# Second attention with its scores formed twice, and the last two experts by token halves

## The chip, the core and the metric

The kernel runs on one core of a Trainium2 chip. That core has a matrix engine (TensorE, PE in the rows, with its weight loads as PEld), a vector engine (VectorE, DVE), an activation engine (ScalarE, ACT), a general engine (GpSimd, POOL) and a queue engine for transfers (SyncE, SP). Each runs its own list of instructions in order and waits on semaphores for the others. The metric is the device time of one execution in microseconds; less is better.

## What is computed

Eight sequences of 128 tokens with 128 channels go through four residual layers: a cross attention with 8 heads, a mixture of 8 experts with 2 chosen per token, a second cross attention with 16 heads of 8 channels, and a three-layer network with weights of +1 and -1. The part that the change is about, from the reference:

```python
def _L1_xattn_ref(x, context, Wq, bq, Wk, bk, Wv, bv, Wo, bo):
    N_HEADS = 16; D_EMBED = 128; D_HEAD = 8
    q = split_heads(x @ Wq + bq)
    k = split_heads(context @ Wk + bk)
    v = split_heads(context @ Wv + bv)
    scores = jnp.einsum('bhqd,bhkd->bhqk', q, k) / np.sqrt(D_HEAD)
    attn = jax.nn.softmax(scores, axis=-1)
    out = jnp.einsum('bhqk,bhkd->bhqd', attn, v)
    return out.transpose(0, 2, 1, 3).reshape(B, S, D_EMBED) @ Wo + bo
x = x + _L0_ffn_ref(_layernorm(x), ...)      # 8 experts, hidden size 256
x = x + _L1_xattn_ref(_layernorm(x), ctx_768, ...)
x = x + _L1_ffn_ref(_layernorm(x), ...)
```

## The kernel before

The program is written by hand, engine by engine: each block lists its engine's instructions in their order, and semaphores join them. Nothing is scheduled by a tool. "Batch" is one sequence of 128 tokens; a "token half" is four batches.

The experts are worked through as 16 pieces q = 0 to 15, expert q // 2 and token half q % 2. TensorE forms the hidden values (`b_hidden`, 12 products of 512 columns), ScalarE applies the SiLU (L895), VectorE multiplies by the gate (`b_gate`, L1212), TensorE goes back to 128 channels (`b_down`, L616), and VectorE adds the result, weighted for each token, to `x_sb` (`b_add`, L1219). In between TensorE forms the keys of the second attention (`k1_keys`), which end in `k_st`: of its 128 rows each head owns 8, each value split into parts (32 rows for a head, so 4 heads in a group `g`, and 4 groups). After the last piece VectorE normalises the four batches of the first half (`ln_root`, `ln_scale`, L1071), TensorE turns them, and `c_queries` forms the queries of four groups for 512 tokens, which ScalarE and VectorE put into `q_all` (`c_query_signed` L936, `c_query_stack` L1302).

The second attention has 32 units, one for each batch and group of four heads. GpSimd spreads the keys of a batch into a block-diagonal form, `k_bd` (`stage_k`, L388), so that one product over all 128 rows gives the scores of four heads (`c_scores`, L693, one of 512 columns). VectorE takes the maximum over the keys (L1311) and subtracts it (L1315), ScalarE takes the exponential (L945), TensorE turns the four 128x128 tiles (`c_turn`, L700), ScalarE copies them out (L950), and TensorE multiplies by the values (`c_values`, L716). The column of ones in `v_a` gives the sum of the exponentials. After four units comes a tail: copy (L955), turn back (L724), division (L1322, L1324), turn (L728), copy (L958), output product (L731), residual and statistics (L1329, L1024). The loop `c_step` works on two batches at a time.

The last network needs a normalised first token half, which GpSimd makes beside the last units (`ln_root` and `ln_scale` on GpSimd, L301 to L316), then `d_unit` (L757) with its evacuations on ScalarE (L981, L987) and VectorE (L1366, L1375). TensorE also has filler products (`keep_clock`, L431: 128x128 products of `ones`), which compute nothing.

## Time and profile before

| | us |
|---|---|
| runs shown, median | 261.87 |
| lowest and highest of the 3 | 260.78 and 262.34 |
| profiled execution, its own time | 261.25 |
| profiled execution, span of the core | 259.5 |

The profile is one execution. Its span is 1.75 us shorter than the time of that same execution; the rest lies around it. TensorE is busy for 92% of the span, VectorE for 73%, ScalarE for 57%, GpSimd for 35%. In the chain of work that ended last, TensorE has 49%, VectorE 27% and ScalarE 8%. By stage, the first attention lies at about 18 to 72 us, the experts at 72 to 157, the second attention at 157 to 232, and the last network reaches to the end. The ends of matrix products are modelled in such a profile, so TensorE looks busy where it may only be draining: starts are safer to read than ends.

### The profile page before, as it was taken

The page shows a single profiled execution, that of the slowest core. Times are in us where ns is not written, and L with a number is a line of the kernel's source. Part 1 is how long each engine was busy: PE and PEld are TensorE (multiplying, and loading weights), DVE is VectorE, ACT ScalarE, POOL GpSimd, SP SyncE. Part 2 cuts the span into 40 slices and gives each one's busy share as a digit, 9 for nine tenths or more (in the row PEclk, how much of TensorE's full clock was granted, in tenths as well). Part 3 has the DMA queues.
Part 4 walks back from the last instruction along what each step waited for, and adds up shares of the span by engine and source line. Part 5 has one row for each costly group of instructions (what it writes and reads, how often), then busy time and mean ns, then how long its engine had stood idle before and what let it go on. Part 6 is the DMA issues. An engine that isn't in the chain of part 4 may idle for free.

```text
span 259.5 us, 5047 instructions
## 1 busy us (share of the span) xinstructions
PE 237.5 (92%) x1726; PEld 185.0 (71%) x1726; DVE 190.7 (73%) x472; ACT 146.8 (57%) x346; POOL 90.4 (35%) x108
## 2 busy tenths in 40 slices
PE   8979798897989999999999999788999998798994
PEld 7346678787967889889889997555655554466782
DVE  0799977776579855655665689977999999568862
ACT  2643968879655432232232144776777777656841
POOL 3352594040402032131269503643655525230200
PEclk9999999999999999999999999999999999999998
DMA  7940010000000012012010000000000000000002
GB/s 200 211 121 4 0 42 3 0 3 0 3 0 3 28 35 61 19 42 61 15 46 23 0 0 1 3 1 3 0 0 3 0 3 0 4 0 0 0 3 81
DMA packets 11243, 6.59 MB, mean 25 GB/s; under 512 B 2772, under 2 KB 10904, under 8 KB 11224
## 3 DMA queue, kind: packets, MB, share of 16 engines
q1 hardware_dynamic: 11224, 6.33, 9.0%
q8 instruction: 12, 0.20, 0.3%
q14 instruction: 7, 0.06, 0.1%
HBM read 5.81 MB, written 0.52 MB: 24 GB/s over the span
## 4 chain that ended last, share of the span: by engine, by line
PE 49%; DVE 27%; issue 8%; ACT 8%; DMA 2%; POOL 2%; DVEq 1%; SPq 0%; ACTq 0%
PE ps L616 10%; PE ps L435 8%; PE ps L437 7%; PE ps L436 7%; PE ps L757 7%; DVE negmax L1311 6%; ACT probs L846 3%; PE ps L526 3%; PE ps L506 3%; DVE xn L1071 2%; DMA x_sb<-in_x 2%; DVE probs L1315 2%; DVE h_c L1302 2%; ACT part L936 1%; DVE stats L1024 1%
## 5 line engine op out<-in xcount | busy, mean ns | idle before, releaser
L895 ACT ACTIVATE kT<-ps 128x512 f32<-128x512 f32 x32 | 19.1, 598 | 43.7 <-PE ps L437 43.6
L388 POOL TENSOR_TENSOR k_bd<-k_st,block_of 128x2048 fp32r<-128x2048 f32 x8 | 28.8, 3602 | 20.1 <-PE ps L693 20.1
L616 PE MATMUL ps<-w,kT 128*128 128x128 f32 x256 | 31.1, 275 | 0.0
L616 PEld LDWEIGHTS ps<-w,kT 128*128 128x128 f32 x256 | 30.4, 192 | 0.7
L1212 DVE TENSOR_TENSOR kT<-ps,kT 128x512 f32<-128x512 f32 x32 | 21.8, 689 | 11.1 <-PE ps L437 8.8
L435 PE MATMUL ps<-xT_hi,w_hi 128*128 128x512 f32 x64 | 26.6, 416 | 0.7 <-issue 0.6
L364 POOL TENSOR_TENSOR w_hi<-w_raw,zero 128x512 fp32r<-128x512 f32 x8 | 8.3, 1040 | 51.6 <-DMA w_raw<-in_L_ffn_W 37.3
L945 ACT ACTIVATE probs<-probs 128x512 f32<-128x512 f32 x32 | 20.0, 629 | 11.0 <-DVE probs L1315 11.0
L437 PE MATMUL ps<-xT_hi,w_lo 128*128 128x512 f32 x64 | 25.2, 393 | 0.0
L436 PE MATMUL ps<-xT_lo,w_hi 128*128 128x512 f32 x64 | 25.0, 390 | 0.0
L1219 DVE SCALAR_TENSOR_TENSOR x_sb<-ps,comb,x_sb 128x128 f32<-128x128 f32 x64 | 18.0, 343 | 9.4 <-PE ps L616 9.4
L1315 DVE TENSOR_TENSOR probs<-ps,negmax 128x512 f32<-128x512 f32 x32 | 22.1, 692 | 3.1
L846 ACT ACTIVATE probs<-ps,negmax 128x128 f32<-128x128 f32 x64 | 22.7, 420 | 1.8 <-DVE negmax L1137 1.8
L700 PE MATMUL ps<-ident,probs 128*128 128x128 f32 x128 | 20.2, 280 | 1.9 <-ACT probs L945 1.6
L1311 DVE TENSOR_REDUCE negmax<-ps 128x4 f32<-128x512 f32 x32 | 21.7, 679 | 0.0
L700 PEld LDWEIGHTS ps<-ident,probs 128*128 128x128 f32 x128 | 14.4, 140 | 7.9 <-ACT probs L945 7.1
L950 ACT ACTIVATE probsT<-ps 128x512 f32<-128x512 f32 x32 | 18.7, 584 | 0.4 <-PE ps L700 0.4
L846 ACT ACTIVATION_READ_ACCUMULATOR probs<-ps,negmax 128x1 f32 x64 | 16.6, 260 | 0.0
L693 PE MATMUL ps<-k_bd,h_c 128*128 128x512 f32 x32 | 15.2, 481 | 0.3 <-DVE h_c L1302 0.3
L435 PEld LDWEIGHTS ps<-xT_hi,w_hi 128*128 128x128 f32 x64 | 12.1, 188 | 3.2 <-issue 0.7
L437 PEld LDWEIGHTS ps<-xT_hi,w_lo 128*128 128x128 f32 x64 | 12.0, 188 | 2.8
L716 PE MATMUL ps<-probsT,qo 128*32 128x128 f32 x256 | 13.6, 285 | 0.4 <-DVE h_c L1302 0.4
(189 smaller groups left out, 533.5 us busy)
## 6 DMA issues: line engine op xcount, KB each, us to landing
w_raw<-in_L_ffn_W SPq DMA_DIRECT2D x16, 128.0 KB, 2.2
w<-in_L_ffn_W SPq DMA_DIRECT2D x8, 128.0 KB, 2.2
x_sb<-in_x SPq DMA_DIRECT2D x1, 512.0 KB, 5.6
out<-qo SPq DMA_DIRECT2D x2, 256.0 KB, 2.3
ctx_sb<-in_ctx SPq DMA_DIRECT2D x1, 384.0 KB, 3.5
w_raw<-in_L_xattn_Wq SPq DMA_DIRECT2D x1, 256.0 KB, 5.8
wo<-in_L_xattn_Wo SPq DMA_DIRECT2D x1, 256.0 KB, 5.6
k_i<-in_L_ffn_k SPq DMA_DIRECT2D x1, 256.0 KB, 3.5
```

The lines of the kernel that those rows point to most:

```text
L388: pool.tensor_tensor(k_bd[:, j, :, :, :], keys, blocks, ALU.mult).then_inc(c_k, 1)
L435: pe.matmul(dst, w_hi, x_hi, start=start, stop=False)
L436: pe.matmul(dst, w_hi, x_lo, start=False, stop=False)
L437: return pe.matmul(dst, w_lo, x_hi, start=False, stop=stop)
L616: ins = pe.matmul(ps[:, 4 + slot, k * C:(k + 1) * C], uT[:, slot, c, k * P:(k + 1) * P], w3[:, buf, c, :], start=(c == 0), stop=(c == NH - 1))
L700: ins = pe.transpose(ps[:, 4 + u % 2, h * P:(h + 1) * P], sh1[:, u % 4, h * P:(h + 1) * P], ident[:, :])
L846: ins = act.activation(probs[:, j, h, :], ps[:, 2 * j + h % 2, (h // 2) * P:(h // 2 + 1) * P], ACT.Exp, bias=negmax[:, j, h:h + 1], scale= ...
L895: act.activation(silu[:, c, :], ps[:, c, :], ACT.Silu).then_inc(b_silu, 1)
L945: act.activation(sh1[:, u % 4, :], sh1[:, u % 4, :], ACT.Exp, scale=D1 ** -0.5).then_inc(c_exp, 1)
L1212: dve.tensor_tensor(uT[:, slot, c, :], ps[:, 2 + c, :], silu[:, c, :], ALU.mult).then_inc(b_u, 1)
L1311: dve.tensor_reduce(negmax1[:, u % 4, :], src, X, ALU.max, negate=True).then_inc(c_max, 1)
L1315: dve.tensor_tensor(sh1[:, u % 4, :].rearrange("p (h k) -> p h k", k=P), src, negmax1[:, u % 4, :].unsqueeze(2).to_broadcast([P, 4, P]), A ...
```

## The change

The second attention forms its scores twice. The first time they have the queries along the partitions; VectorE reduces them only to the maximum. The negated maxima are placed in `top_w` (zero elsewhere), TensorE turns `top_w`, and VectorE adds the result to the queries: the maximum thus stands as one further row of each head, and the keys have 1.0 in that row. The second product has the keys along the partitions, gives the shifted and already turned scores, and ScalarE writes their exponential straight to where the value product reads it. Block-diagonal keys, subtraction, turning and copy of the exponentials are gone. To free the row, the repeated weights of the queries and keys are zero in one of the four parts (`NS - 1`).

Both score products work on 32 rows at a time, so the head's own rows, at `tile_position` (32r, 0); a "half" `a` is two of the four heads of every group, 8 products of 128 columns, in order g, r, so that two row groups take turns and write to different banks.

The loop over the steps `s` is new on all engines. In step `s` TensorE forms the shifted scores of batch `s`, the first scores of batch `s + 2`, turns the maxima of batch `s + 1`, multiplies values of batches `s - 1` and `s`, and does parts of the tails of `s - 1` and `s - 2`. Two banks hold first scores, two hold shifted scores.

The last two experts, 6 and 7, are worked through as: 6 on the first half, 7 on the first half, 6 on the second half, 7 on the second half. The core of the diff:

```diff
-            def stage_k(b, j):
-                keys = f32(k_st[:, :, bass.ds(b * P, P)]).unsqueeze(2).to_broadcast([P, NG, 4, P])
-                blocks = block_of[:, :].unsqueeze(1).unsqueeze(3).to_broadcast([P, NG, 4, P])
-                pool.tensor_tensor(k_bd[:, j, :, :, :], keys, blocks, ALU.mult).then_inc(c_k, 1)
...
+            pool.memset(top_w, 0.0).then_inc(zeros_ok, 1)
...
+                    pe.wait_ge(b_lo, E)
+                    b_hidden(i * 4 + 5, 1, 0)
...
             b_down(q, 0, 0, NP - 1)
-            pe.wait_ge(b_lo, E)
-            b_hidden(q + 2, 1, 0)
-            b_down(q + 1, 1, 0, NP - 1)
-            b_down(q + 2, 0, 1, NP - 1)
+            b_hidden(q + 2, 0, 1)
+            b_down(q + 1, 1, 1, NP - 1)
             b_hidden(q + 3, 1, 1)
-            keep_clock(5, M0 + 1)
+            b_down(q + 2, 0, 0, NP - 1)
             b_down(q + 3, 1, 1, NP - 1)
...
-                pe.matmul(ps[:, g, :], q, k_bd[:, j, g, :, :].rearrange("p h k -> p (h k)"),
-                          start=True, stop=True).then_inc(c_s, 1)
...
+                for g in range(NG):
+                    for r in (2 * a, 2 * a + 1):
+                        rows, bs = slice(32 * r, 32 * r + 32), slice(b * P, (b + 1) * P)
+                        ins = pe.matmul(ps[:, S_BANK + r % 2, g * P:(g + 1) * P], q_all[rows, g, bs], k_st[rows, g, bs],
+                                        start=True, stop=True, tile_position=(32 * r, 0))
...
+            def c_shifted(b, a):
+
+                if a == 0:
+                    pe.wait_ge(c_qa, b + 1)
+                if 2 * b + a > 0:
+                    pe.wait_ge(c_exp, 2 * b + a)
...
+                        ins = pe.matmul(ps[:, E_BANK + r % 2, g * P:(g + 1) * P], k_st[rows, g, b * P:(b + 1) * P],
+                                        q_sh[rows, b % 2, g * P:(g + 1) * P], start=True, stop=True,
+                                        tile_position=(32 * r, 0))
...
+            def c_step(s):
+                if s < NB:
+                    c_shifted(s, 0)
+                if s + 2 < NB:
+                    c_scores(s + 2, 0)
+                if s == 0:
+                    c_queries(NG + 2)
+                if s + 1 < NB:
+                    c_turn_max(s + 1)
+                if s >= 2:
+                    c_tail(s - 2, 1)
+                if 1 <= s <= NB:
+                    c_values(s - 1, 1)
+                if s == NB:
+                    d_unit(0)
+                if s < NB:
+                    c_shifted(s, 1)
+                if s + 2 < NB:
+                    c_scores(s + 2, 1)
+                if s < NB:
+                    c_values(s, 0)
...
+            def c_exp_half(b, a):
+                act.wait_ge(c_st, 2 * b + a + 1)
+                act.activation(p1T[:, a, :, :, :].rearrange("p r g q -> p r (g q)"), ps[:, E_BANK:E_BANK + 2, :], ACT.Exp,
+                               scale=D1 ** -0.5).then_inc(c_exp, 1)
...
                 dve.wait_ge(masks, 8)
+                dve.tensor_scalar(is_lo[:, 1:2], is_lo[:, 1:2], 1.0, None, ALU.is_equal).then_inc(masks, 1)
...
+            def c_top(b, a):
+
+                dve.wait_ge(c_s, 2 * b + a + 1)
+                top = top_w[:, b % 2, :, :].rearrange("p g (r m) -> p r g m", r=4)[:, 2 * a:2 * a + 2, :, 3 * D1]
+                dve.tensor_reduce(top, ps[:, S_BANK:S_BANK + 2, :].rearrange("p r (g k) -> p r g k", g=NG), X, ALU.max,
+                                  negate=True).then_inc(c_max, 1)
+
+            def c_shift(b):
+
+                dve.wait_ge(c_w, b + 1)
+                dve.tensor_tensor(q_sh[:, b % 2, :].rearrange("p (g q) -> p g q", g=NG),
+                                  ps[:, W_BANK, :].rearrange("p (g q) -> p g q", g=NG),
+                                  f32(q_all[:, :, b * P:(b + 1) * P]), ALU.add).then_inc(c_qa, 1)
```

VectorE at the end of the experts, before: L1219 is `b_add` (four for a piece), L1212 `b_gate`, L1024 the statistics, L1071 the normalised tokens.

```order
L1212 TENSOR_TENSOR kT<-ps,kT 128x512 x2
L1219 SCALAR_TENSOR_TENSOR x_sb<-ps,comb,x_sb 128x128 x8
L1024 BN_STATS stats<-x_sb 128x6 x4
L1212 TENSOR_TENSOR kT<-ps,kT 128x512 x2
L1038 BN_AGGR meanvar<-stats 128x2 x4
...
L1071 TENSOR_SCALAR xn<-x_sb,meanvar,rs 128x128 x4
L1219 SCALAR_TENSOR_TENSOR x_sb<-ps,comb,x_sb 128x128 x4
```

The same place now (L1251 is `b_add`, L1244 `b_gate`, L1054 the statistics, L1101 the normalised tokens):

```order
L1244 TENSOR_TENSOR kT<-ps,kT 128x512 x2
L1251 SCALAR_TENSOR_TENSOR x_sb<-ps,comb,x_sb 128x128 x4
L1054 BN_STATS stats<-x_sb 128x6 x4
L1244 TENSOR_TENSOR kT<-ps,kT 128x512 x2
L1068 BN_AGGR meanvar<-stats 128x2 x4
...
L1251 SCALAR_TENSOR_TENSOR x_sb<-ps,comb,x_sb 128x128 x4
L1101 TENSOR_SCALAR xn<-x_sb,meanvar,rs 128x128 x4
L1251 SCALAR_TENSOR_TENSOR x_sb<-ps,comb,x_sb 128x128 x4
```

One addition of a piece has moved from before the statistics to between the root and the normalised tokens.

TensorE in the steady part of the attention, before, one batch: L693 scores, L700 turns of the exponentials, L716 values, L731, L724 and L728 the tails.

```order
L693 MATMUL ps<-k_bd,h_c 128x512
L700 MATMUL ps<-ident,probs 128x128 x4
L716 MATMUL ps<-probsT,qo 32x128 x4
L731 MATMUL ps<-wo,o1T 128x128
L693 MATMUL ps<-k_bd,h_c 128x512
...
L724 MATMUL ps<-ident,ov 128x128 x4
```

The same place now, one step: L701 shifted scores, L688 first scores, L714 turns of the maxima, L729 values, L746, L742 and L754 the tails.

```order
L701 MATMUL ps<-h_a,k_st 128x128 x8
L688 MATMUL ps<-k_st,h_c 128x128 x8
L714 MATMUL ps<-ident,probs 128x128 x4
L746 MATMUL ps<-ident,o 128x128
L729 MATMUL ps<-probsT,qo 32x128 x8
L701 MATMUL ps<-h_a,k_st 128x128 x8
L688 MATMUL ps<-k_st,h_c 128x128 x8
L729 MATMUL ps<-probsT,qo 32x128 x8
L742 MATMUL ps<-ident,ov 128x128 x4
L754 MATMUL ps<-wo,o1T 128x128
```

Of a batch's 4 score products, 16 turns of exponentials and 16 value products, 32 score products of 32 rows, 4 turns of maxima and 16 value products remain. Each fence above counts instructions as written; a full-precision product of 128 columns shows as two in the rows.

VectorE in the same step now: L1342 the maxima of a half, L1348 the shift, L1356 and L1360 the division, L1366 the residual.

```order
L1342 TENSOR_REDUCE probs<-ps 128x2x4
L1348 TENSOR_TENSOR h_a<-ps,h_c 128x512
L1342 TENSOR_REDUCE probs<-ps 128x2x4
L1356 RECIPROCAL rsum<-ps 128x16
L1360 TENSOR_TENSOR o<-ps,rsum 128x4x4x8
L1366 TENSOR_TENSOR x_sb<-ps,x_sb 128x128
L1054 BN_STATS stats<-x_sb 128x6
```

Before, the same stretch held four pairs of maximum and subtraction:

```order
L1311 TENSOR_REDUCE negmax<-ps 128x4
L1315 TENSOR_TENSOR probs<-ps,negmax 128x512
...
L1322 RECIPROCAL rsum<-ps 128x16
L1324 TENSOR_TENSOR o<-ps,rsum 128x128
...
L1329 TENSOR_TENSOR x_sb<-ps,x_sb 128x128
```

## Rows read from the trace of the kernel before

**Rows 1.** The page: span and busy time of each engine

```profile
span 259.5 us, 5047 instructions
...
PE 237.5 (92%) x1726; PEld 185.0 (71%) x1726; DVE 190.7 (73%) x472; ACT 146.8 (57%) x346; POOL 90.4 (35%) x108
```

**Rows 2.** Two stages: length, busy us of PE, PEld, DVE, ACT, POOL, clock

```profile
163.00:183.00 20.00, 16.89 (x130) 11.26 (x129) 16.40 (x27) 14.26 (x27) 9.90 (x13) 1.00 0.00 1
183.00:215.00 32.00, 30.29 (x292) 18.12 (x290) 29.28 (x60) 24.39 (x48) 14.67 (x5) 1.00 0.00 1
```

**Rows 3.** Chain that ended last: start us, duration us, what

```profile
198.03 0.29 DVE x_sb L1329
...
204.72 0.29 DVE x_sb L1329
```

**Rows 4.** Groups by line: count | busy us, mean ns | idle before

```profile
L388 POOL TENSOR_TENSOR k_bd<-k_st,block_of 128x2048 fp32r<-128x2048 f32 x8 | 28.8, 3602 | 20.1 <-PE ps L693 20.1
...
L1315 DVE TENSOR_TENSOR probs<-ps,negmax 128x512 f32<-128x512 f32 x32 | 22.1, 692 | 3.1
...
L1311 DVE TENSOR_REDUCE negmax<-ps 128x4 f32<-128x512 f32 x32 | 21.7, 679 | 0.0
...
L945 ACT ACTIVATE probs<-probs 128x512 f32<-128x512 f32 x32 | 20.0, 629 | 11.0 <-DVE probs L1315 11.0
...
L950 ACT ACTIVATE probsT<-ps 128x512 f32<-128x512 f32 x32 | 18.7, 584 | 0.4 <-PE ps L700 0.4
...
L1137 DVE TENSOR_REDUCE negmax<-ps 128x8 f32<-128x1024 f32 x8 | 9.8, 1223 | 4.7 <-PE ps L494 4.6
...
L981 ACT ACTIVATE k_bd<-ps,scale 128x512 fp32r<-128x512 f32 x8 | 5.4, 692 | 4.3 <-PE ps L757 4.3
```

**Rows 5.** TensorE in order of time: start us, duration us, instruction

```profile
202.16 0.48 PE L693 MATMUL ps<-k_bd,h_c 128*128 128x512 f32 x1
202.48 0.60 PE L700 MATMUL ps<-ident,probs 128*128 128x128 f32 x4
203.01 0.43 PE L716 MATMUL ps<-probsT,qo 128*32 128x128 f32 x8
203.36 0.49 PE L731 MATMUL ps<-wo,o1T 128*128 128x128 f32 x2
```

**Rows 6.** TensorE in order of time, first attention

```profile
47.31 1.16 PE L494 MATMUL ps<-kT,qo 64*128 64x128 f32 x16
48.40 0.33 PE L517 MATMUL ps<-probsT,v 128*64 128x128 f32 x2
```

**Rows 7.** All engines in order of time, first queries

```profile
163.88 1.90 PE L431 MATMUL ps<-ones 128*128 128x128 f32 x16
...
164.74 0.74 DVE L1302 SCALAR_TENSOR_TENSOR h_c<-ps,is_lo,part 128x512 fp32r<-128x512 f32 x1
```

**Rows 8.** Order of time, end of the experts

```profile
145.98 3.74 PE L616 MATMUL ps<-w,kT 128*128 128x128 f32 x32
...
152.59 0.69 DVE L1212 TENSOR_TENSOR kT<-ps,kT 128x512 f32<-128x512 f32 x1 [0.21 <-PE ps L437]
...
155.59 1.41 DVE L1071 TENSOR_SCALAR xn<-x_sb,meanvar,rs 128x128 f32<-128x128 f32 x4
...
156.92 1.11 DVE L1219 SCALAR_TENSOR_TENSOR x_sb<-ps,comb,x_sb 128x128 f32<-128x128 f32 x4
```

**Rows 9.** Order of time, end of the attention

```profile
215.64 0.17 DVE L1047 TENSOR_SCALAR rs<-nt 128x4 int32<-128x4 int32 x1
...
218.80 3.15 POOL L316 TENSOR_SCALAR xn<-x_sb,meanvar,rs 128x128 f32<-128x128 f32 x4
...
231.96 0.29 DVE L1024 BATCH_NORM_STATS2 stats<-x_sb 128x6 f32<-128x128 f32 x1
...
233.01 0.69 DVE L1375 TENSOR_TENSOR k_bd<-kT,k_bd 128x512 fp32r<-128x512 f32 x1
```

**Rows 10.** Order of time, the masks before the experts

```profile
79.40 0.17 DVE L1120 TENSOR_SCALAR sign<-is_lo 128x3 f32<-128x3 f32 x1
```

More of the change, by code:

```diff
@@ L199, in program @@
         stored = sem("stored")
-        const_ok, split_w0, split_w1, masks = (sem(n) for n in (
-            "const_ok", "split_w0", "split_w1", "masks"))
+        const_ok, zeros_ok, split_w0, split_w1, masks = (sem(n) for n in (
+            "const_ok", "zeros_ok", "split_w0", "split_w1", "masks"))
         pool_step = sem("pool_step")
@@ L636, in _, with b_pair @@
             b_hidden(1, 0, 1, (1,))
-            with pe.Fori(0, NP - 1) as i:
+            def b_pair(i, last):
                 b_down(i * 4, 0, 0, i)
@@ new lines, in c_turn_max, with c_values @@
+            def c_turn_max(b):
+                pe.wait_ge(c_max, 2 * b + 2)
+                if b >= 1:
+                    pe.wait_ge(c_qa, b)
+                if b >= 4:
+                    pe.wait_ge(c_x, b - 3)
+                for g in range(NG):
+                    ins = pe.transpose(ps[:, W_BANK, g * P:(g + 1) * P], top_w[:, b % 2, g, :], ident[:, :])
+                ins.then_inc(c_w, 1)
+            def c_values(b, a):
+                pe.wait_ge(c_exp, 2 * b + a + 1)
+                if a == 0:
@@ L780, in _ @@
-            pe.wait_ge(masks, 12)
+            def c_step(s):
[19 more added lines that the diff above has]
+                    c_values(s, 0)
+                if s == 0:
+                    c_queries(NG + 3)
+                if 1 <= s <= NB:
+                    c_tail(s - 1, 0)
+                if s == NB - 1:
+                    ln_transposes(3, 0)
+                if s >= NB:
+                    d_unit(2 * (s - NB) + 1)
+                if s >= 2:
+                    c_tail(s - 2, 2)
+                if s == NB:
+                    d_unit(2)
@@ L911, in _ @@
             b_silu_step(1)
-            act.wait_ge(masks, 9)
+            act.wait_ge(masks, 10)
             k1_signed(0, 0)
@@ L935, in c_query_signed @@
                     act.wait_ge(k1_st, NK1 - 1 + n)
-                act.activation(part[:, n % 2, :], ps[:, n if n < NG else M0 + 1, :], ACT.Copy,
+                act.activation(part[:, n % 2, :], ps[:, q_bank(n), :], ACT.Copy,
                                scale=sign[:, 0:1]).then_inc(c_part, 1)
@@ L960, in c_step @@
-            def c_step(p, first, last):
-                for u in range(8):
-                    if u < 3 and not first:
-                        c_tail(p * 2 - 1, 1, u)
-                    if 4 <= u < 7:
-                        c_tail(p * 2, 0, u - 4)
-                    if not (last and u + 2 >= 8):
-                        c_exp_unit(p, u + 2)
-                    if not (last and u == 7):
-                        c_turn_copy(p, u + 1)
-                    if first and u < 4:
-                        c_query_signed(NG + u)
-                    if last and u == 4:
-                        ln_hi_copy(3, 0)
+                    act.activation(o1T[:, :], ps[:, t_bank(b), 0:P], ACT.Copy).then_inc(c_oT, 1)
@@ new lines, in c_step @@
+            def c_step(s):
+                if s < NB:
+                    c_exp_half(s, 0)
+                if s == 0:
+                    c_query_signed(NG + 2)
+                if 1 <= s <= NB:
+                    c_tail(s - 1, 0)
+                if s == NB:
+                    d_evacuate(0)
+                if s >= 2:
+                    c_tail(s - 2, 1)
+                if s < NB:
+                    c_exp_half(s, 1)
+                if s == 0:
+                    c_query_signed(NG + 3)
+                if s == NB - 1:
+                    ln_hi_copy(3, 0)
+                if s == NB:
+                    d_evacuate(1)
+                    d_evacuate(2)
@@ L1333, in c_step @@
-            def c_step(p, first, last):
-                for u in range(8):
-                    if u < 4 and not first:
-                        c_tail(p * 2 - 1, 1, u)
-                    if u >= 4:
-                        c_tail(p * 2, 0, u - 4)
-                    if not (last and u + 3 >= 8):
-                        c_shift(p, u + 3)
-                    if first and u < 4:
-                        c_query_stack(NG + u)
-                    if last and u == 0:
-                        ln_seed_pool(3, 0)
-                    if last and u == 4:
-                        ln_low(3, 0)
```

310 lines of the change are left out of this document (145 added, 165 removed).

## The prediction, made before the changed kernel ran

> **What bounds the kernel now.** I read the page first: of 259.5 us TensorE is busy 237.5, VectorE 190.7 [rows 1]. That average hides the attention, so next I read the stages: from 183 to 215 us VectorE is busy 29.3 of 32, ScalarE 24.4, and TensorE shows 30.3 with modelled ends, at full clock (1.00) [rows 2]. Who paces it is in the chain that ended last: it runs through VectorE's maxima, and the residual of one batch follows that of the batch before by 204.72 - 198.03 = 6.69 us [rows 3]. Four units of a maximum (679 ns) and a subtraction (692 ns) [rows 4] are 5.5, the tail on VectorE is the other 1.2. So VectorE bounds the steady part. In TensorE's own order of time I look at starts, since those are measured: scores to turns 0.32, turns to values 0.53, values to the next kind 0.35 [rows 5], together 1.20 for a unit; that is 4.8 for four units, and about 0.7 for the tail. TensorE could do 5.5 where VectorE needs 6.69.
>
> **The experts.** TensorE's work is the same; 8 of its products (`b_down` of piece 14, half of the 3.74 us pair) [rows 8] move from before the last hidden piece to behind it, so that piece ends 1.8 us earlier, and the 10 fillers there go. The last gate ended at 152.59 + 0.69 = 153.28 [rows 8] and now ends near 151.5. The statistics root follows on VectorE as before (2.3 us, from there to the normalised tokens at 155.59 [rows 8]). But the addition of piece 14, 1.11 us [rows 8], now stands between the root and these tokens, as the order shows. Net 1.7 - 1.1 = **0.6 us earlier**. The 1.11 is hidden nowhere: it is on the chain. Expert 7's split weights are wanted one hidden piece earlier; GpSimd splits them as soon as the fourth-last piece allows, some 7 us ahead, so that costs nothing, and if it did, at most one hidden piece. The third mask costs one more small operation on VectorE ahead of the gating, 0.17 us [rows 10] with its hand-off; the copy behind it shrinks by a quarter: **0.1 us later**. GpSimd's new clearings of `top_w` and of the weights' fourth part are far ahead of their readers, in time in which GpSimd stands idle; without that cover they would cost under 1 us each.
>
> **A step in the steady part.** Two prices aren't in the trace. First the half of 8 products on 32 rows. A product of 128 columns in this operand type, alone on all rows, starts every 0.107 us: 16 fillers take 1.90 with the last one's 0.28 [rows 7]. Two row groups that take turns do overlap: the first attention's scores on 64 rows, which in full precision cost 0.107 an entry on one group, show 16 entries in 1.16, a start each 0.056 [rows 6]. So 8 products start within 0.39 and end at 0.67. Lower end: half, if the row group were freed after 128 columns at 2.4 GHz (0.2); upper end: no overlap, 8 x 0.107 = 0.86. I take 0.056 a product, since rows 6 is the same pattern of two groups. Going over to another shape of product costs: 47.31 + 15 x 0.056 = 48.15 is the last start, the next kind starts at 48.40, so 0.25 after it [rows 6].
>
> The Trainium skill speaks against hoping for the lower end: in "TensorE: Matmul & The Clock Gate", section on LDWEIGHTS, the load takes as long for 32 rows as for 128, one column a cycle at 1.2 GHz, and overlaps running products only in another row group. Fillers at 0.107 a start agree with it. By the lower end a step of TensorE would lose another 0.7 us and VectorE would pace it; by the rule it does not.
>
> Second the exponential of 1024 columns out of the matrix memory. 512 columns are 629 ns, and ScalarE's copy from that memory 584 [rows 4]; twice 629 is the upper end, 629 the lower; I take 1.1. The maximum of 1024 columns is known, 1223 ns, from the first attention; the shift is like the subtraction, 692 [rows 4].
>
> TensorE's step then: shifted half and first half, 15 x 0.056 + 0.25 = 1.09; turns of maxima and of the tail, 5 x 0.107, to the values 0.53; 16 full-precision entries of values on 4 column groups, twice the 0.21 of one set plus 0.14 for leaving [rows 5] = 0.56; again 1.09; again 0.56; the tail, 6 entries of 0.107 and 0.1 = 0.74. **Sum 4.57, say 4.6 us** against 6.69.
>
> Do its waits fit? From the step's start: first scores of a half done at 1.12, their maximum at 2.37; TensorE wants that at 2.64. The turned maxima are there at 1.7, the shift done at 2.97, wanted at 4.6. The second scores are done at 3.31, maximum at 4.56, wanted at 5.05. The first exponential runs from 0.70 to 1.8, wanted at 2.19; the second, behind the two copies of the tails, from 2.9 to 4.0, wanted at 4.6. VectorE adds up to 2 x 1.14 + 0.61 + 1.2 = 4.1 (an instruction follows the one before about 0.09 before its shown end). All slacks are positive but small, 0.25 to 0.6. Stages of spreading keys on GpSimd (3.6 us a batch [rows 4]) were hidden and give nothing.
>
> **Filling the pipeline.** Before, the fourth query stacking ended at 164.74 + 0.74 = 165.48 [rows 7], held up 1.3 us by the first unit, which VectorE did ahead of it; now it comes straight after the third, and 0.6 earlier: 163.65. From there nothing overlaps at first: scores 0.67, maximum 1.22, scores, maximum, turns 0.66, shift 0.69, with six hand-offs of 0.05 that is 5.4, to 169.0. Then VectorE has six maxima (6.8), two shifts (1.4) and the four remaining stackings (4 x 0.75 = 3.0) until step 2 begins: 11.2 us, and 2.4 of waits, of which the largest, 1.2, is for the last queries behind their copy. Step 2 begins at **182.6**.
>
> **Draining it.** Steps 2 to 5 are full, 4.6 each: step 5 begins at 196.4. The first half's last residual comes 5.7 into it, the seed of the root one more later, 203.1. Before, GpSimd's root and normalised tokens took from 215.64 + 0.17 to 218.80 + 3.15, 6.1 us [rows 9]; now 203.1 + 6.1 = 209.2. TensorE, with two lighter steps (3.7 and 3.4), is there at 208.1, so this GpSimd chain, hidden before, is now what ends last, by 1.1. Behind it turns, copy and low part (0.3, 0.6, 0.7 and queueing) give the first unit of the last network at 212.1. ScalarE then has five evacuations of 692 ns [rows 4] and two small copies in one row before the last tail's product: 216.0. Product, residual and statistics: 217.2, and one evacuation with its low part, 1.45 us: **218.7**. The same low part ended at 233.01 + 0.69 = 233.70 before [rows 9]. From there the two kernels are alike: root, tokens, last layers.
>
> Sum: 233.7 - 218.7 = 15.0 us earlier, in which the experts' 0.6 is contained, less 0.1 for the masks: 14.9. The profiled execution's own time is 261.25, so **246.4 us**. It lies 0.6 below the median of the runs shown, 261.87, so I don't scale.
>
> **Rivals.**
> (A) The forecast with its sizes: 242.5 to 251.5. Speaking for it, every chain fits within the step. Its low end is VectorE pacing at 4.2 with shorter waits at the fill; its high end a step of 5.3, where small slacks turn into waits: four full steps count, 4 x 0.7 = 2.8, and 2 more at the fill. 0.84.
> (B) The row groups don't overlap. Each half costs 0.47 more, 4 in a step: 6.5 us, barely under 6.69. Over four full steps 7.5, the lighter steps and the fill another 3 to 4: 257 to 258. For it: the trace has two groups only on 64 rows. Against it: rows 6 is plain. 0.08.
> (C) The first scores and their maxima play ping-pong: the two banks of first scores are single, so TensorE, which works in order, stands before each half until VectorE is done, and with it the shifted half queued behind. If every half waits, the step is 2 x (0.67 + 1.22 + 0.1) + the shift 0.7 + the tail 1.2 = 5.9: 1.3 x 4 = 5.2 more, 252 to 253. 0.04.
> (D) Slower: TensorE's clock. The granted clock was 1.00 in both stages [rows 2]; if with quarter-array products and gaps of 1 to 2 us in the fill it fell to the lower of its levels, 1.2 instead of 2.4 GHz, TensorE's products of a step, 4.6 less about 0.9 of changes of shape, would double: 8.3 us. Four full steps give 15, two lighter ones and the fill another 6: 267. It turns slower from a step of about 6.6 us, all else as forecast, with the fill in proportion. Against it: in the stage with TensorE busy 16.9 of 20 us, the clock held. 0.03.
> (E) It does nothing measurable, as some mixture of B and D in part: 0.01.
>
> **How the numbers follow.** The likeliest is A, 246.4. 242.5 to 251.5 holds 0.84 of the chance; B, C and D lie above. A measurement of this kernel can tell about 0.5% (1.3 us) from no change. Faster by more: A, B, C, 0.96, less what of B comes out near 260, 0.01: 0.95; within: 0.02; slower: 0.03.
>
> **What would show it.** In the changed profile: the normalised tokens of the first half start near 155.0, half a microsecond before 155.59; the shifted halves start 0.056 apart; residuals of successive batches follow each other by 4.6 in the middle; GpSimd's tokens end near 209 with TensorE waiting about 1 us for them; the statistics of the last batch end near 217.2. A step over 5.3, starts 0.107 apart, or a granted clock below 1.00 between 163 and 210 would make it wrong.

## The result, and the profile after

The changed kernel takes 255.3 us (median of 4 runs, 254.9 to 255.7) where the kernel before took 261.4 beside it: a ratio of 0.9745, 95% interval 0.971 to 0.978. It is faster, as forecast, but by 6.1 us and not by 15; 255.3 lies above the range of 242.5 to 251.5. The profiled execution is one of 254.9 us.

The page of the changed kernel, span, busy time and the clock's row of the 40 slices:

```profile
span 253.1 us, 5075 instructions
...
PE 233.8 (92%) x1834; PEld 192.1 (76%) x1834; DVE 173.5 (69%) x433; ACT 127.6 (50%) x298; POOL 62.9 (25%) x103
...
PEclk9998999999999999999999999955699999899999
```

Beside [rows 1] VectorE lost 17 us of work, ScalarE 19, GpSimd 27.5, all of which the change meant to save. The news is in the last row. In slices 27 to 29 TensorE's granted clock reads 5, 5 and 6 tenths, and there is a dent in slice 35 (and a small one in slice 4, on which more at experiment 6). Before, both stages of the attention stood at 1.00 [rows 2]. The same stage by 2 us windows shows where it begins and ends (columns: length, busy us and count of PE, PEld, DVE, ACT and POOL, then the clock):

```profile
162.00:164.00 2.00, 0.37 (x2) 0.01 (x1) 1.68 (x3) 0.98 (x2) 1.42 (x8) 1.00 0.00 0
164.00:166.00 2.00, 1.97 (x14) 1.90 (x14) 1.21 (x1) 1.65 (x4) 1.30 (x4) 0.64 0.03 8
166.00:168.00 2.00, 2.00 (x14) 1.79 (x13) 0.77 (x2) 0.00 (x1) 0.62 (x2) 0.50 0.00 0
...
178.00:180.00 2.00, 2.00 (x8) 1.48 (x7) 1.23 (x1) 0.50 (x1) 0.00 (x0) 0.50 0.00 0
180.00:182.00 2.00, 2.00 (x17) 1.58 (x17) 0.82 (x2) 0.69 (x1) 0.00 (x0) 0.59 0.00 0
182.00:184.00 2.00, 2.00 (x28) 1.33 (x26) 1.70 (x2) 1.02 (x1) 0.00 (x0) 1.00 0.01 4
```

In the first window TensorE works 0.37 of 2 us. Then the clock goes to 0.50, 1.2 instead of 2.4 GHz, and stays there some 17 us, in which every window has TensorE busy 2.00 of 2 us but the first (1.97). TensorE in order of time has the gap and what the low clock does to a half of 8 products, and in the last three lines how long a step is once the clock is back:

```profile
164.03 0.66 PE L688 MATMUL ps<-k_st,h_c 32*128 32x128 f32 x8 [1.66 <-DVE h_c L1334]
164.62 1.54 PE L425 MATMUL ps<-ones 128*128 128x128 f32 x6
166.09 1.11 PE L688 MATMUL ps<-k_st,h_c 32*128 32x128 f32 x8
...
202.76 0.66 PE L701 MATMUL ps<-h_a,k_st 32*128 32x128 f32 x8
203.26 0.61 PE L688 MATMUL ps<-k_st,h_c 32*128 32x128 f32 x8
...
207.49 0.66 PE L701 MATMUL ps<-h_a,k_st 32*128 32x128 f32 x8
```

Steps 2 to 5 begin at 188.57, 193.30, 198.03 and 202.76, and the next at 207.49: 4.73 us each, where [rows 3] had 6.69 and the forecast 4.6. So the steady part came out. Step 2 begins 6.0 us later than the 182.6 forecast, and from step 5 to the end of the last low part another 1.9 are lost. There TensorE in order of time has a second stall:

```profile
217.44 0.48 PE L782 MATMUL ps<-xT_hi,d_w 128*128 128x512 f32 x1 [0.67 <-DVE xT_lo L1108]
217.76 0.40 PE L782 MATMUL ps<-xT_lo,d_w 128*128 128x512 f32 x1
219.77 1.08 PE L742 MATMUL ps<-ident,ov 128*128 128x128 f32 x4 [1.61 <-ACT o1T L991]
```

ScalarE in the same place:

```profile
218.19 0.69 ACT L1020 ACTIVATE h_a<-ps,scale 128x512 fp32r<-128x512 f32 x1 [0.75 <-PE ps L782]
218.78 0.68 ACT L1026 ACTIVATE kT<-ps,scale 128x512 f32<-128x512 f32 x1
219.35 0.28 ACT L991 ACTIVATE o1T<-ps 128x128 f32<-128x128 f32 x1
```

TensorE's turn of the last tail waits for batch 6's `o1T`, a copy of 0.28 us that ScalarE has queued behind the first unit's two copies. The clock falls again behind it, to 0.50 from 220 to 222.

**The account.** The low part that ended at 233.70 before [rows 9] now ends at 226.28 + 0.69 = 226.97; 218.7 was forecast.

```profile
226.28 0.69 DVE L1410 TENSOR_TENSOR h_a<-kT,h_a 128x512 fp32r<-128x512 f32 x1
```

The 8.3 us between are 6.0 until step 2, 0.4 in three steps of 4.73 for 4.6, and 1.9 from there on. The profiled execution as a whole came 8.5 us above the forecast (254.9 for 246.4), so nearly all of the miss lies in these three. The experiments ask for the cause of the first and the last.

### The profile page after: what moved, and what is told of

The parts are those of the page before. It is cut to its first block, busy times and chain, and to the rows that moved or that the text cites. A ratio compares the mean times of both kernels' runs of the same rounds, so it can differ in the third digit from the quotient of the medians.

```text
span 253.1 us, 5075 instructions
## 1 busy us (share of the span) xinstructions
PE 233.8 (92%) x1834; PEld 192.1 (76%) x1834; DVE 173.5 (69%) x433; ACT 127.6 (50%) x298; POOL 62.9 (25%) x103
## 4 chain that ended last, share of the span: by engine, by line
PE 71%; DVE 13%; ACT 7%; issue 4%; DMA 2%; POOL 2%; SPq 0%; DVEq 0%
PE ps L429 9%; PE ps L610 9%; PE ps L782 9%; PE ps L431 8%; PE ps L430 8%; PE ps L688 4%; ACT probs L883 3%; PE ps L520 3%; PE ps L701 3%; PE ps L500 3%; DMA x_sb<-in_x 2%; PE ps L729 2%; PE ps L425 2%; PE ps L436 2%; PE ps L714 2%
## 5 line engine op out<-in xcount | busy, mean ns | idle before, releaser
L1244 DVE TENSOR_TENSOR kT<-ps,kT 128x512 f32<-128x512 f32 x32 | 21.8, 689 | 11.1 <-PE ps L431 8.8
L1251 DVE SCALAR_TENSOR_TENSOR x_sb<-ps,comb,x_sb 128x128 f32<-128x128 f32 x64 | 18.0, 343 | 8.6 <-PE ps L610 8.5
L1342 DVE TENSOR_REDUCE probs<-ps 128x8 f32<-128x1024 f32 x16 | 19.6, 1225 | 6.0 <-PE ps L688 6.0
L982 ACT ACTIVATE probsT<-ps 128x1024 f32<-128x1024 f32 x16 | 16.4, 1027 | 8.8 <-PE ps L701 8.8
L312 POOL TENSOR_TENSOR nt<-rs 128x4 f32<-128x4 f32 x3 | 0.6, 198 | 53.7 <-DVE rs L1077 53.7
L430 PEld LDWEIGHTS ps<-xT_lo,w_hi 128*128 128x128 f32 x64 | 12.1, 189 | 2.0
L688 PE MATMUL ps<-k_st,h_c 32*128 32x128 f32 x128 | 11.8, 309 | 1.7 <-DVE h_c L1334 1.7
L1054 DVE BATCH_NORM_STATS2 stats<-x_sb 128x6 f32<-128x128 f32 (+1 forms) x32 | 7.6, 283 | 8.0 <-DMA x_sb<-in_x 7.7
L1169 DVE TENSOR_REDUCE negmax<-ps 128x8 f32<-128x1024 f32 x8 | 9.8, 1223 | 4.7 <-PE ps L488 4.6
L1181 DVE TENSOR_TENSOR probs<-probs,rsum 128x1024 f32<-128x1024 f32 x8 | 12.4, 1552 | 0.3
L688 PEld LDWEIGHTS ps<-k_st,h_c 32*128 32x128 f32 x128 | 10.1, 220 | 3.2 <-issue 2.4
```

Of the source, the lines that this page charges most:

```text
L430: pe.matmul(dst, w_hi, x_lo, start=False, stop=False)
L688: ins = pe.matmul(ps[:, S_BANK + r % 2, g * P:(g + 1) * P], q_all[rows, g, bs], k_st[rows, g, bs], start=True, stop=True, tile_position=(3 ...
L982: act.activation(p1T[:, a, :, :, :].rearrange("p r g q -> p r (g q)"), ps[:, E_BANK:E_BANK + 2, :], ACT.Exp, scale=D1 ** -0.5).then_inc(c_ ...
L1244: dve.tensor_tensor(uT[:, slot, c, :], ps[:, 2 + c, :], silu[:, c, :], ALU.mult).then_inc(b_u, 1)
L1251: ins = dve.scalar_tensor_tensor(x_sb[:, b, :], ps[:, 4 + slot, k * C:(k + 1) * C], comb[:, bass.ds(e, 1), b:b + 1].rearrange("p o b -> p ...
L1342: dve.tensor_reduce(top, ps[:, S_BANK:S_BANK + 2, :].rearrange("p r (g k) -> p r g k", g=NG), X, ALU.max, negate=True).then_inc(c_max, 1)
```

## The experiments

The theory: TensorE's clock fell because the fill left TensorE idle or nearly so, and it costs some 6 us in the fill and 1 in the drain. The rivals: it falls whatever fills the stretch (the cause is elsewhere), or the new products of 32 rows themselves bring it down. "Fillers" are the products on `ones` of `keep_clock`, whose result nobody reads: `keep_clock(n, bank)` issues 2n of 128 columns. The changed kernel has two groups of 6 in its fill, where the kernel before had one of 16.

**1. One gap filled.**

```
             for n in range(NG):
                 c_queries(n)
+            keep_clock(8, M0)
             pe.wait_ge(k1_st, NK1)
             c_scores(0, 0)
```

> The changed kernel with 16 filler products put behind the first four query products, where TensorE stood idle for 1.7 us. Theory 1 (the clock): the pipeline's fill took 6.0 us longer than forecast because TensorE's granted clock fell to 0.50 right behind that idle stretch and stayed there for 17 us. Then the clock stays at 1.00, the first shifted scores of batch 2 start near 183 instead of 188.6, and the time is 249.5 to 250.5 instead of 255.3. Theory 2 (the waits of the fill were too short in the forecast, the clock only shows the idle time): the time stays within 0.7 of 255.3.

Measured: 254.8 us (254.1 to 255.3), ratio to before 0.9755, interval 0.974 to 0.977, which can't be told from the changed kernel's. The 1.66 us gap is gone, and the clock is down all the same, only later (windows as above):

```profile
164.00:166.00 2.00, 1.60 (x16) 1.31 (x15) 1.11 (x1) 1.57 (x4) 1.30 (x5) 1.00 0.00 0
166.00:168.00 2.00, 1.83 (x16) 1.76 (x17) 1.24 (x2) 0.49 (x2) 0.70 (x2) 0.79 0.00 0
168.00:170.00 2.00, 2.00 (x12) 1.67 (x13) 1.16 (x3) 0.19 (x1) 0.00 (x0) 0.50 0.00 0
```

The time went as theory 2 had it and the mechanism as neither: that gap alone is not the cause, since without it the clock fell later and stayed low for some 13 us. But TensorE still stood idle further on, before the second half of the first scores:

```profile
166.17 0.66 PE L688 MATMUL ps<-k_st,h_c 32*128 32x128 f32 x8 [0.57 <-DVE probs L1343]
```

**2. ScalarE's copy moved, in the drain.** The `o1T` copy of batch 6 goes ahead of the first unit's copies:

```
+                if s >= 2 and s != NB + 1:
+                    c_tail(s - 2, 1)
                 if s == NB:
                     d_evacuate(0)
-                if s >= 2:
+                if s == NB + 1:
                     c_tail(s - 2, 1)
```

> The changed kernel with one exchange on ScalarE: in step 8 the small copy of batch 6's tail stands ahead of the two evacuations of the network's first unit instead of behind them. Theory 1 (a wait that the forecast overlooked: the turning of batch 7 waits for that copy, and TensorE stands for 1.6 us and drops to a clock of 0.50 for 2 to 3 us): 1.5 to 2.5 us less than 255.3, no clock below 1.00 between 216 and 226. Theory 2 (ScalarE is full there anyway, so that what moves ahead delays something else by as much): within 0.7 of 255.3.

Measured: four executions, 252.5, 253.9, 277.3 and 279.4 us. The first two are 1.4 to 2.8 below the changed kernel; there is no interval. In the other two the mean granted clock was 0.864 and 0.843, for 0.956 and 0.958; they come up again with the rivals below. In the trace of the 252.5 the stall of 1.61 us is gone (the first unit at 218.03, the turn right behind it) and the clock reads 1.00 from 206 to 246:

```profile
218.03 0.47 PE L782 MATMUL ps<-xT_hi,d_w 128*128 128x512 f32 x1 [0.66 <-DVE xT_lo L1110]
218.34 0.39 PE L782 MATMUL ps<-xT_lo,d_w 128*128 128x512 f32 x1
218.57 0.60 PE L742 MATMUL ps<-ident,ov 128*128 128x128 f32 x4
```

**3. The experts' part alone**, added to the kernel before: the last two experts by token halves, the attention as it was.

> The kernel before with only the experts' part of the change: the last two experts by token halves. Theory 1 (the forecast's term): 0.4 to 0.6 us less than 261.4. Theory 2 (worth nothing, since the addition moved behind the root takes the gain): within 0.2 of 261.4.

Measured: 260.6 us (260.3 to 261.3, 10 runs), ratio 0.9965, interval 0.994 to 0.999, so 0.9 us (0.4 to 1.5). The term of 0.6 stands, and the experts have no part in the missing 9 us. The order of the experts came here without the third mask, whose 0.1 us no run prices by itself.

**4. The kernel before without its fillers.**

```
-            keep_clock(8, M0 + 1)
             c_turn(0, 0)
             ln_transposes(2, 1)
```

> The kernel before without its 16 filler products behind the first three units' scores. If idle TensorE time of 1.5 to 2 us at this place lets the clock fall whatever the attention's form, the clock falls to 0.50 here too between 163 and 180, and the time is 3 to 6 us above 261.4. If the fall belongs to the new form (products on 32 rows), the clock stays at 1.00 and the time within 0.7 of 261.4.

Measured: 263.05 us (6 runs, 262.4 to 264.9), ratio 1.0071, interval 1.005 to 1.009: 1.5 us more by the medians, 1.9 by the ratio, where 3 to 6 were expected. In its trace (the execution of 264.9) TensorE waits 1.57 us where the fillers [rows 7] were, and the clock follows, without one product of the new form in the kernel:

```profile
167.84 0.63 PE L700 MATMUL ps<-ident,probs 128*128 128x128 f32 x4 [1.57 <-ACT probs L944]
```

```profile
168.00:170.00 2.00, 1.98 (x9) 1.04 (x8) 1.93 (x4) 1.92 (x6) 1.69 (x4) 0.67 0.03 8
170.00:172.00 2.00, 1.22 (x6) 1.03 (x6) 1.87 (x4) 1.43 (x3) 1.61 (x1) 0.50 0.00 0
```

Here it was back at 1.00 by 176, after some 6 us, and the price was 1.5 to 1.9 us. VectorE paced this kernel, which is the likely reason for the low price; in the changed one TensorE paces (experiment 12), and its clock was down 17 us.

**5. The fill filled densely**, with experiment 2's exchange kept:

```
             for n in range(NG):
                 c_queries(n)
+            keep_clock(8, M0)
             pe.wait_ge(k1_st, NK1)
             c_scores(0, 0)
-            keep_clock(3, M0)
+            keep_clock(7, M0)
             c_scores(0, 1)
             ln_transposes(2, 1)
-            keep_clock(3, M0)
+            keep_clock(5, M0)
             c_turn_max(0)
```

> The changed kernel with 16 fillers behind the first four queries, 14 and 10 in place of 6 and 6 further on (between the halves of batch 0's first scores and ahead of its turn), and ScalarE's o1T copy ahead of the first unit's copies. Theory 1 (the clock falls because TensorE sat idle around the first scores; in the last experiment one gap of 0.57 us was left at 165.6 and the fall came at 167.5): no gap is left, the granted clock reads 1.00 all through 160 to 190, step 2 begins near 183 in place of 188.6, the residual chain ends about 8 us earlier, 247 (246.4 to 248.5). Theory 2 (the clock falls in this stretch whatever fills it, because so much of it is products with 32 rows in the load, or for a cause outside the stretch): the clock falls to 0.50 again and the time is that of the version with ScalarE's exchange alone, 252.5 to 253.5.

Measured: the profiled execution took 246.24 us, and another 247.9. Two more took 257.05 and 278.4 with a mean granted clock of 0.945 and 0.858, for 0.989 and 0.984 in the first two, so the median, 252.5, is a mixture of both and says little. The profiled one by windows, and behind it TensorE in order of time:

```profile
162.00:164.00 2.00, 2.00 (x20) 1.88 (x18) 1.61 (x3) 0.92 (x2) 1.41 (x7) 1.00 0.00 0
164.00:166.00 2.00, 2.00 (x22) 1.93 (x21) 1.23 (x1) 1.65 (x4) 1.37 (x4) 1.00 0.00 0
166.00:168.00 2.00, 2.00 (x22) 1.85 (x21) 1.03 (x1) 0.45 (x1) 0.57 (x2) 1.00 0.00 0
```

```profile
182.88 0.66 PE L701 MATMUL ps<-h_a,k_st 32*128 32x128 f32 x8
...
187.60 0.66 PE L701 MATMUL ps<-h_a,k_st 32*128 32x128 f32 x8
```

TensorE is busy 2.00 in each of these windows, and the clock is 1.00 from 22 us until past the last product. Step 2 begins at 182.88, forecast 182.6, and the whole kernel takes what was forecast, 246.4. The second rival, that it falls whatever fills the stretch, is out: in the changed kernel and in experiments 1 and 2 it had fallen in all 12 executions (mean clock 0.966 or lower). What is left is that the same order held the clock in some executions and not in others.

**6. More fillers later in the fill**: as 5, with `keep_clock(3, M0)` at three more places (behind the sixth query, and in step 0 ahead of the second shifted half and of the values; the expectation counts one place too many).

> As the one before, with 6 more fillers each in four places of the last part of the fill: behind the sixth query, and in step 0 ahead of the second half of the shifted scores and ahead of the values. Theory 1: nothing more to win if the clock already holds, the same 247, or up to 1 us more where the fillers stand on the path; if the version before lets the clock fall late in the fill, this one holds it. Theory 2: 253 to 255.

Measured: 247.8 us (247.3 to 249.5 where the clock held, one execution of five at 255.9), ratio 0.946, interval 0.943 to 0.949. Nothing is won over 5 by these, as theory 1 said. The profiled execution is the 249.5. Its clock holds in the fill too, but is low earlier, in slice 4:

```profile
PEclk9995999999999999999999999999999999999999
```

That is a stretch near 17 to 26 us, behind a wait of TensorE for VectorE's `ctxT_lo`. Nine of the fourteen profiled executions have it, of both kernels and whatever the fill. A short one (some 4 us) costs nothing that can be seen: the tokens behind the experts start at 155.12 in experiment 5 with it and at 155.07 in experiment 12 without. The longer one here costs 1.6 us (they start at 156.73). So a mean granted clock of 0.984 to 0.987 can come from there alone, and the mean says something of the fill only where it is clearly lower.

**7. The same fillers with 32 rows.** As 5, but the fillers of the three places are products of the new form, two for each full one:

```
+            def keep_clock32(n, bank):
+                for i in range(4 * n):
+                    r = 32 * (i % 2)
+                    pe.matmul(ps[:, (bank, 5)[i % 2], 0:P], ones[r:r + 32, 0:1].to_broadcast([32, P]), ones[r:r + 32, :],
+                              start=True, stop=True, tile_position=(r, 0))
```

> As the first of these, with each 128-row filler of the three places replaced by two fillers with 32 rows in the load, alternating between two row groups, so that the stretch is filled for as long but with the products of the new form. If it is idle time alone that lowers the clock: 1.00 throughout and the time of the first of these, 247. If products of 32 rows count for less than full ones: the clock falls to 0.50 around 164 to 168 and the time is 252.5 to 254.

Measured: 253.7 us (five executions of 253.5 to 256.2, the sixth 278.0), ratio 0.969, interval 0.966 to 0.971. The mean granted clock of the five is 0.966, 0.966, 0.965, 0.944 and 0.965, and of the sixth, the profiled one, 0.857: it fell in every one. In that trace TensorE's queue was as full as in 5:

```profile
164.00:166.00 2.00, 2.00 (x40) 2.00 (x38) 1.23 (x1) 1.65 (x4) 1.39 (x5) 1.00 0.00 0
166.00:168.00 2.00, 2.00 (x20) 1.60 (x20) 1.23 (x1) 0.54 (x1) 0.39 (x1) 0.68 0.00 0
```

So idle time is not the whole of it. Here products of 32 rows held the clock less well than full ones.

**8. The same exchange in the kernel before**: its 16 fillers replaced by 32 of the new form.

> The kernel before, with its 16 fillers at 163.9 (128 rows) replaced by 32 fillers of 32 rows in two row groups, which fill as long. Without these fillers it was 1.3 to 1.9 us slower, with 6 us at the low clock. If products of 32 rows keep the clock up as well as full ones: 261.4 to 261.9 and 1.00 throughout. If they count for less: the clock falls near 168 and the time is 262.5 to 263.3, as without fillers.

Measured: 261.8 us (11 runs), ratio 0.9987, interval 0.996 to 1.001: no change. The clock read 0.993 or more in nine executions and 0.974 in two (264.6 and 265.2 us); without any fillers (experiment 4) it was 0.974 to 0.987 in all six. So this went the way that the expectation gave to "as well as full ones", and it contradicts a simple reading of 7. Products of 32 rows are no idle time. They carried 1.9 us behind products of 512 columns, and didn't carry the changed kernel's fill, where the real work between them is of 32 rows and 128 columns as well. In the one trace of this version, the 264.6, the clock fell at 168 right behind them, with TensorE never idle there, and it had been low at 18 to 26 us too.

**9. Fillers of 512 columns**, for as long:

```
+            def keep_clock512(n, bank):
+                for _ in range(n):
+                    pe.matmul(ps[:, bank, :], ones[:, 0:1].to_broadcast([P, P]), ones[:, 0:1].to_broadcast([P, TG]), start=True, stop=True)
```

They are 8, 7 and 5 in the three places of experiment 5 (the expectation was written for 7, 6 and 4), and `keep_clock(4, M0 + 1)` instead of 3 ahead of the first turns of the tokens.

> The densely filled version with its fillers in the three places exchanged for products of 512 columns (7, 6 and 4 of them for 16, 14 and 10 of 128 columns, TensorE filled for as long), and one filler pair more at 155.2. Same order, same waits. Where the 128-column fillers stood, the clock held in most executions and fell in some. If how little of the time products really stream (idle time, 32-row products and short ones alike) is what decides: the clock holds in nearly all of them, 246.0 to 247.0. If only idle time decides: no difference from the 128-column fillers, that is 246 to 248 with falls in about one execution of four.

Measured: **247.05 us** (246.6 to 248.3, 6 runs), ratio 0.944, interval 0.941 to 0.947, mean clock 0.998 or more in five executions and 0.986 in one. TensorE in order of time: 8 of them fill the time of 16 short ones, each streaming four times the columns.

```profile
162.65 1.91 PE L429 MATMUL ps<-ones 128*128 128x512 f32 x8
164.49 0.66 PE L692 MATMUL ps<-k_st,h_c 32*128 32x128 f32 x8
165.08 1.79 PE L429 MATMUL ps<-ones 128*128 128x512 f32 x7
```

This version beats both kernels.

**10. The same without the extra pair at 155.2.**

> The version with 512-column fillers (they are 8, 7 and 5 in the three places, as in the kernel that ran) without its one other difference, the extra filler pair at 155.2. If the 512 columns of the fillers are what keeps the clock up: 246.2 to 247.5 with no fall in any execution. If it was the pair at 155.2 that filled the last idle 0.3 us: falls come back in about one execution of four, as with the 128-column fillers.

Measured: 247.8 us (246.2 to 248.1, 5 runs), ratio 0.946, interval 0.943 to 0.948, clock 0.984 to 0.999. "No fall in any execution" was a miss: the profiled one has a short fall, which ends by itself.

```profile
174.00:176.00 2.00, 2.00 (x12) 1.54 (x11) 1.65 (x2) 0.67 (x1) 0.00 (x0) 0.61 0.00 0
176.00:178.00 2.00, 2.00 (x15) 1.56 (x15) 0.80 (x2) 0.69 (x1) 0.00 (x0) 0.54 0.00 0
178.00:180.00 2.00, 2.00 (x30) 1.44 (x28) 1.77 (x2) 1.02 (x1) 0.00 (x0) 1.00 0.01 4
```

In the 20 executions with the three places filled by 128 columns (experiments 5, 6, 11 and 12) the mean clock was 0.963 or lower, and the time 255.9 us or more, in six; in the 11 with 512 columns the mean was never below 0.984 and the time never above 248.3. (Two more of the 20, both of experiment 11, read 0.979 and 0.980; the early stretch and the dip behind the drain's stall are together large enough for that.) Six in 20 beside none in 11 would come by chance about once in twenty times, so that 512 columns hold the clock better is likely and not shown. Whether the pair at 155.2 does anything, 5 against 6 executions don't tell.

**11. The drain's price with the clock held before it**: as 5, without ScalarE's exchange.

> The densely filled version without ScalarE's exchange in step 8: the changed kernel with more fillers in the fill, and nothing else. It prices the drain's stall with the clock held before it: TensorE waits 1.6 us for the o1T copy behind the first unit's copies and the clock dips behind it, which in the changed kernel came to 2.3 us against the forecast. Theory: 2 to 2.5 above the densely filled version with the exchange, 248.5 to 249.2 where the fill's clock holds. Rival (ScalarE's exchange only moves the wait): 246.2 to 247.2.

Measured: 251.6 us (248.0 to 258.6), a mixture again. The profiled one had the clock up in the fill, 247.96 us, 1.7 above the one of experiment 5, a little less than the 2 to 2.5 expected. The stall is back and the clock has no dip behind it this time:

```profile
214.12 0.63 PE L742 MATMUL ps<-ident,ov 128*128 128x128 f32 x4 [1.61 <-ACT o1T L992]
...
219.32 0.69 DVE L1411 TENSOR_TENSOR h_a<-kT,h_a 128x512 fp32r<-128x512 f32 x1
```

The low part ends at 219.32 + 0.69 = 220.01, and in experiment 5 at 217.62 + 0.69 = 218.31:

```profile
217.62 0.69 DVE L1413 TENSOR_TENSOR h_a<-kT,h_a 128x512 fp32r<-128x512 f32 x1
```

From step 5's start (197.09, 197.06 and 202.76) it is 22.9 here, 21.2 with the exchange, and 24.2 in the changed kernel. So 1.7 is ScalarE's order and 1.3 the clock's dip behind it, from one execution of each; 22.3 was forecast.

**12. Who paces the step.** As 5, with 4 fillers more in four steps:

```
+                if 3 <= b <= 6:
+                    keep_clock(2, W_BANK)
                 for g in range(NG):
                     ins = pe.transpose(ps[:, W_BANK, g * P:(g + 1) * P], top_w[:, b % 2, g, :], ident[:, :])
```

> As the first of these, with 4 fillers more in each of steps 2 to 5, ahead of the turn of the maximum (0.43 us of TensorE each). Theory of the prediction (TensorE paces the new step, 4.73 us of it): each of these four steps takes 5.1 to 5.2 and the time is 1.6 to 2.0 us above the first of these. Rival (the ring over VectorE's maximum, the turn, the shift and the exp sets the step, TensorE has slack there): steps stay within 0.15 of 4.73 and the time within 0.6.

Measured: the profiled execution is the one of five in which the clock fell in the fill (256.5 us), but the steady part has it at 1.00. The starts of its shifted halves there:

```profile
191.24 0.66 PE L701 MATMUL ps<-h_a,k_st 32*128 32x128 f32 x8
...
196.44 0.66 PE L701 MATMUL ps<-h_a,k_st 32*128 32x128 f32 x8
...
201.63 0.66 PE L701 MATMUL ps<-h_a,k_st 32*128 32x128 f32 x8
```

5.20 a step for 4.73, all of the added 0.47 (four starts 0.107 apart, and what entering and leaving them costs). TensorE paces the new step and has no slack. The median is 248.3 us, 2.0 above experiment 5's profiled execution and 0.3 above its other one with the clock up. So the lengths of the steps decide here, and the times, with so few of experiment 5, don't.

## Why the prediction was right or wrong

**The experts** [rows 8]: right. Forecast 0.6 less 0.1 for the masks, measured 0.9 with 0.4 to 1.5 as its interval. (Its own terms, a gate 1.8 earlier less 1.1, give 0.7.) In the changed kernel the tokens start at 155.19, forecast near 155.0.

**The step in the steady part**: right. Forecast 4.57, measured 4.73, and paced by TensorE (experiment 12). Term by term, from the starts in one step: the two halves in a row 1.04 (1.09 forecast, from [rows 6]), the values 0.57 (0.56), the tail 0.81 (0.74), the turns with a turn of the tail 0.70 (0.53, where the change of shape between them was left out). The exponential of 1024 columns, the one price taken between wide ends, is 1027 ns (1.1), and the maximum 1225 (1223):

```profile
L1342 DVE TENSOR_REDUCE probs<-ps 128x8 f32<-128x1024 f32 x16 | 19.6, 1225 | 6.0 <-PE ps L688 6.0
...
L982 ACT ACTIVATE probsT<-ps 128x1024 f32<-128x1024 f32 x16 | 16.4, 1027 | 8.8 <-PE ps L701 8.8
```

Two row groups do overlap: rival B is out, and rival C too, since no half waited for VectorE's maximum in the steady steps.

**Filling the pipeline**: this step failed. "scores 0.67, maximum 1.22, scores, maximum, turns 0.66" was summed at 2.4 GHz all through. The chain itself was right, for with the clock held (experiment 5) step 2 begins at 182.88, forecast 182.6. But by the same sum TensorE works for two halves of 0.67 and the turns' 0.66 in 5.4 us and stands for the other 3.4, in the very place where the kernel before had 16 fillers [rows 7]; the sum took them for nothing, and the working never asked what they were there for. At 1.2 GHz step 2 begins at 188.57: 5.7 us of the 8.3 missing are the clock in the fill, from one execution of either version.

**The rival that came true in part** is D. It names the place and the cause, "with quarter-array products and gaps of 1 to 2 us in the fill", and got 0.03. Two readings misled. The argument against it, that the clock held in the stage with TensorE busy 16.9 of 20 us [rows 2], is about the kernel with the fillers in it, and experiment 4 shows that without them it does not hold there. And D was priced for the clock low to the end, 267, so that the case between, low in the fill and back in the steady part, had no rival at all; it gives 6 us more than A, 252 to 253, and stood outside the range. One sum of D is wrong as well: for the whole 14.9 us to go, with the fill in proportion, a step must be near 7.3 (14.9 shared by 4 steps and the 1.6 steps' worth of fill is 2.7 each on 4.6), and not 6.6.

D also came true entirely, in four executions: the two of experiment 2 and one each of 5 and 7, at 277.3 to 279.4 us, slower than the kernel before. The trace of experiment 7's has the clock down from the fill to 241 us, and its steps are 202.93 - 194.38 = 8.55 us long, D's 8.3:

```profile
PEclk9979999999999999999999995555555555599999
194.38 1.11 PE L707 MATMUL ps<-h_a,k_st 32*128 32x128 f32 x8
...
202.93 1.11 PE L707 MATMUL ps<-h_a,k_st 32*128 32x128 f32 x8
```

Its 267 was too low because fill and drain cost some 20 us more than in experiment 5 there (11.5 and 8.8), where D had 6 for the fill and two light steps. What makes one execution recover after 17 us and another not at all, no run here shows.

**Draining it**: wrong by 1.9. The phrase "five evacuations of 692 ns [rows 4] and two small copies in one row before the last tail's product" prices ScalarE's queue by its length, and misses that TensorE's turn of the last tail waits for the `o1T` copy of the batch before, which stands in that queue behind `d_evacuate(0)`. That costs 1.7, and the clock's dip behind it 1.3; the rest of the term was 1.1 too large (21.2 with both gone, for 22.3). The length itself was right: with the exchange the last tail's product starts at 215.72, 3.97 after the first unit at 211.75, and 3.9 was forecast. The 1.1 lies ahead of that unit. TensorE was to wait about 1 us for GpSimd's tokens; in experiment 5 these end at 209.79, TensorE comes to their turn at 209.26 without a stop on its queue, and the first unit follows 1.96 after them, forecast 2.9.

**The sign and the size.** With the clock held and ScalarE's copy in its place (experiment 5) the rebuilding is worth the 15 us that were forecast, 261.25 to 246.24 in one execution of each; by experiment 9's six runs it is 14.6 (13.8 to 15.5). That 246.24 falls on the forecast's 246.4 is in part luck, since the errors of size in it nearly cancel. Of these the changed kernel gives back 7.0 to the clock (5.7 and 1.3) and 1.7 to the order; 0.3 in the fill and 0.4 in the steps are errors of size, and 1.1 of the drain's estimate was too much. That makes the 8.3 of the account.

## What to carry to other kernels

Work that a rebuilding takes away from TensorE's stretches of waiting is work that may have kept its clock up: where a kernel has fillers, find out what they hold, and lay new ones into every wait of the new order before its time is summed at the full clock. When TensorE becomes the engine that paces, a fall of the clock can cost more than while another paced (here 5.7 us for 1.5 to 1.9), so a rival that has the clock low for a part of the stretch needs a price of its own. And a queue is to be read instruction by instruction for who waits on each, not by its length: a copy of 0.28 us behind 1.2 us of others cost 1.7.

## What the runs showed of the hardware

- The clock went to its low level within 0.6 us of TensorE's return from 1.66 us of idleness (changed kernel), and behind 1.57 us (experiment 4). It fell as well with no gap over 0.35 us in the 12 us before (experiment 12's profiled execution), and it held after 1.96 us at 15 to 17 us (experiment 9's). So no length of gap decides by itself. The Trainium skill, "TensorE: Matmul & The Clock Gate", section on the HAM clock gate, has a rule against idle gaps that speaks of longer ones than any of these. Taken alone it would have had none of these falls; the traces don't agree with it, and they decide.
- How long the clock stays low varies widely: 17 us in the changed kernel, 6 in experiment 4, 3 in the profiled execution of experiment 10, over 70 in experiment 7's, with TensorE busy 2.00 of 2 us in nearly every window.
- The same instructions, at the same times within 0.05 us up to 166.2, ended at 1.00 in one execution and at 0.68, then 0.50, in another (the two programs differ only from step 2 on). This row, of experiment 12's profiled execution, stands against the one of experiment 5 at the same time:

```profile
166.00:168.00 2.00, 2.00 (x17) 1.81 (x17) 1.02 (x1) 0.00 (x0) 0.53 (x2) 0.68 0.00 0
```

- Fillers of 128 columns and of 512 keep the queue as full, and yet the first had a long fall in 6 of 20 executions and the second in none of 11 (a short one in experiment 10's profiled execution). Why 32-row fillers held the clock in the kernel before (9 of 11) and didn't in the new one (0 of 6) stays open.
